# The expert stage of a graph, mixer and mixture-of-experts block, rebuilt around one table of turns

## What is computed

```python
# N = 1250 tokens, D = 768, G*E = 32 experts, M = 384; two groups of the 4, two experts of each
glog = xf @ Wg + bg                       # top 2 of 4 groups, softmax of their logits
elog = take_along_axis(elog_all, gidx)    # top 2 of 8 experts in each, softmax again
comb[n, expert] = ggate * egate           # 4 of 32 entries of a token are not zero
h = gelu(x[n] @ W1[e] + b1[e])            # for the tokens of an expert
out = sum_e comb[n, e] * (h @ W2[e] + b2[e])
```

## Time and profile before

| | us |
|---|---|
| three runs, median (lowest to highest) | 2640.47 (2627.52 to 2644.08) |
| profiled execution, first to last instruction | 2648.0 |
| of it from the first real `ex_PH` to the last | 563.3 |

### The profile page before, as it was taken

One profiled execution on the slowest core, in us unless ns is written; L12 is line 12 of the kernel. 1 busy time (PEld: TensorE's weight loads), 2 busy tenths in 40 slices (PEclk: granted clock), 3 DMA queues, 4 the chain that ended last, 5 costly groups with the idle time before them and its releaser, 6 DMA issues. The chain is left out here.

```text
span 2648.0 us, 32969 instructions
## 1 busy us (share of the span) xinstructions
PE 2149.9 (81%) x8696; PEld 1415.3 (53%) x8697; DVE 1172.5 (44%) x2660; ACT 443.9 (17%) x721; POOL 190.2 (7%) x205
## 2 busy tenths in 40 slices
PE   2998998596999922599999799539846888988997
PEld 1666665452555512488888455215543555555554
DVE  3113213133666626579888011056434444444442
ACT  1232112100111112122222000000000222222221
POOL 0000000000000000000000000000001222222222
PEclk9998998897999955799999899769956999989999
DMA  4001200113000045222322411321152777778653
GB/s 162 40 0 63 81 0 36 70 44 117 23 23 24 22 150 184 112 111 95 115 99 81 161 62 55 130 80 48 31 206 81 207 210 225 219 240 257 163 122 66
DMA packets 104535, 278.90 MB, mean 105 GB/s; under 512 B 8053, under 2 KB 53159, under 8 KB 103067
## 3 DMA queue, kind: packets, MB, share of 16 engines
q1 hardware_dynamic: 82727, 210.86, 22.6%
q0 software_dynamic: 15184, 55.37, 9.1%
q10 hardware_dynamic: 6560, 11.86, 1.2%
HBM read 214.49 MB, written 63.57 MB: 105 GB/s over the span
## 5 line engine op out<-in xcount | busy, mean ns | idle before, releaser
L1179 PE MATMUL gat_Z<-h,gat_wt 125*125 125x256 f32 (+1 forms) x1600 | 356.4, 382 | 40.0 <-DVE gat_wt L1095 40.0
L1179 PEld LDWEIGHTS gat_Z<-h,gat_wt 125*125 125x125 f32 x1600 | 299.3, 189 | 85.7 <-DVE gat_wt L1095 40.5
L2034 PE MATMUL ex_PH<-ex_w,ex_xT 128*128 x636 | 240.3, 532 | 24.2 <-DVE ex_xT L1883 14.5
L542 PE MATMUL mix_G<-mix_w,mix_xs 128*125 128x384 f32 x720 | 243.4, 489 | 0.0
L2023 PE MATMUL ex_PY<-ex_w,ex_hT 128*128 (+1 forms) x660 | 223.7, 489 | 15.9 <-POOL ex_hT L1838 14.8
L825 PE MATMUL count_G<-gnn_w,xnT 128*125 (+1 forms) x480 | 214.3, 596 | 18.5 <-issue 18.5
L1329 PE MATMUL gat2p_Y<-gat2p_w,gat2p_hT 128*125 128x384 f32 x640 | 209.3, 491 | 12.2 <-DMA gat2p_w<-in_L_gnn_W 12.2
L2034 PEld LDWEIGHTS ex_PH<-ex_w,ex_xT 128*128 128x128 f32 x636 | 126.9, 207 | 109.7 <-issue 48.2
L2023 PEld LDWEIGHTS ex_PY<-ex_w,ex_hT 128*128 128x128 f32 x660 | 126.1, 191 | 105.0 <-issue 18.8
L542 PEld LDWEIGHTS mix_G<-mix_w,mix_xs 128*125 128x125 f32 x720 | 133.4, 189 | 85.1 <-issue 2.6
L1329 PEld LDWEIGHTS gat2p_Y<-gat2p_w,gat2p_hT 128*125 128x125 f32 x640 | 121.3, 190 | 99.8 <-issue 14.9
(11 more groups left out here) (292 smaller groups left out, 2456.9 us busy)
## 6 DMA issues: line engine op xcount, KB each, us to landing
ex_w<-in_L_ffn_W SPq DMA_DIRECT2D x64, 1152.0 KB, 8.0
gat_cnt<-c_dram SPq DMA_DIRECT2D x50, 610.4 KB
h1T_dram<-gat_oT ACTq DMA_DIRECT2D x40, 250.0 KB, 2.0
gat2p_hT<-h1T_dram SPq DMA_DIRECT2D x10, 1000.0 KB, 4.8
mix_w<-in_L_mix_qkv_w SPq DMA_DIRECT2D x6, 1152.0 KB
ct_dram<-count_out SPq DMA_DIRECT2D x40, 157.0 KB, 2.2
mix_w_slice<-in_L_gnn_W SPq DMA_DIRECT2D x6, 1024.0 KB, 11.0
gat2p_w<-in_L_gnn_W SPq DMA_DIRECT2D x4, 1536.0 KB, 13.7
```

The lines of the kernel that those rows point to most:

```text
L542: last = pe.matmul(G[c][:], xs[b][:, k, :], w[:, k, c, :], start=(k == 0), stop=(k == KD - 1))
L1179: last = pe.matmul(Z[b][j][:], wt[b][:, s, :], h[:, s, bass.ds(hd, 1), j * HC:(j + 1) * HC + j], start=(s == 0), stop=(s == NT - 1))
L2034: last = pe.matmul(PH[:], xT[:, k, :], w1[:, bass.ds(b, 1), k, :], start=(k == 0), stop=(k == KD - 1))
```

## The change

- `route_phase` makes a table of turns once, by small products on PE in a new PSUM tile `TB`: for each turn the expert (`etab`) and the offset of its first place (`offs`), and the number of turns (`total`). The nine chained DVE steps that made `ntile` and `tstart` go, and so do two copies into `codes`, which POOL now makes.
- First product: the weights `w1` are held still, 128 by 128, and the 128 tokens of `xT` stream. Eighteen matmuls of 128 columns take the place of six of 384. The result is already turned, so that the transposes `ex_TH` and their copy go; ACT takes Gelu straight from PSUM with the bias as a column per partition (`b1T`, loaded once), in three pieces.
- `find` works by the table: one DVE operation makes `Q` from `posm` and `offs`, with the expert loaded into a register (`etab`). Row numbers and gates are kept in four slots each (`ids`, `gate`).
- DVE, ACT and POOL have one loop over all turns, in place of loops over experts. POOL issues the gather of turn i+2 ahead of the scatter of turn i. Before, it issued the scatter first.
- A first activation `warm` loads ACT's table once. The host stores `W1`, `W2` and `b1` in the order in which a partition reads them.

The core of the diff, with the new programs of the engines in `expert_phase`:

```diff
+            def gather(n):
+                pool.wait_ge(idx_ready, n + 1)
+                if not (isinstance(n, int) and n == 0):
+                    pool.wait_ge(x_turned, n)
+                    pool.wait_ge(gathered, n * 16)
...
+            def scatter(n):
+                pool.wait_ge(y_d, n + 1)
+                pool.wait_ge(y_a, n + 2)
+                pool.wait_ge(idS_ready, n + 1)
...
+            with pool.Fori(0, end) as i:
+                gather(i + 2)
+                scatter(i)
...
+            def find(n):
+                e = expert_of(dve, n)
...
+                    dve.wait_ge(ids_done, n)
+                dve.scalar_tensor_tensor(Q[:], posm[:, :, bass.ds(e, 1)].to_broadcast([P, NT, SLOT]),
+                                         offs[:, bass.ds(at, 1)],
+                                         iot[:].unsqueeze(1).to_broadcast([P, NT, SLOT]),
+                                         ALU.subtract, ALU.is_equal).then_inc(q_ready, 1)
+
+            def indices(n):
+                slot = slot_of(dve, n)
+                dve.wait_ge(ids_done, n + 1)
+                dve.wait_ge(y_a, n)
+                dve.tensor_copy(cod[:], PI[:]).then_inc(ids_copied, 1)
+                dve.wait_ge(ids_copied, n + 1)
+                dve.scalar_tensor_tensor(gate[:, slot], cod[:, 5:6], cod[:, 4:5], cod[:, 3:4], ALU.add, ALU.add)
...
+            with dve.Fori(0, end) as i:
+                indices(i + 2)
+                find(i + 3)
+                turn_x(i + 1)
+                second(i)
...
             def second(n):
-                act.wait_ge(gemm2, n)
-                act.wait_ge(g_ready, n)
-                act.activation(y[:, 384:768], PY[1][:], ACT.Copy, scale=gS[:]).then_inc(y_a, 1)
...
+                slot = slot_of(act, n)
+                act.wait_ge(idx_ready, n + 1)
+                act.wait_ge(added, n * 16)
+                act.wait_ge(gemm2, n + 1)
+                act.activation(y[:, 384:768], PY[1][:], ACT.Copy, scale=gate[:, slot]).then_inc(y_a, 1)
+
+            act.wait_ge(consts, 2)
+            act.activation(warm[:], pad[:], ACT.Gelu)
+            act.sem_inc(h_gelu, KM)
+            act.sem_inc(y_a, 1)
...
+            with act.Fori(0, end) as i:
+                first(i)
+                turn_x(i + 1)
+                second(i)
...
+            def first(n, b):
+                pe.wait_ge(xT_d, n + 1)
+                pe.wait_ge(xT_a, n + 1)
+                for m in range(KM):
+                    pe.wait_ge(h_gelu, n * KM + (m + 1))
+                    for k in range(KD):
+                        last = pe.matmul(PH[m][:], w1[:, b, k, m * 128:(m + 1) * 128], xT[:, k, :],
+                                         start=(k == 0), stop=(k == KD - 1))
+                    last.then_inc(gemm1, 1)
...
+                        with pe.Fori(0, count) as _:
+                            n = pe.snap(turn)
+                            find(n + 2)
+                            first(n, b)
+                            turn_x(n + 1)
+                            second(n, b)
+                            pe.reg_add(turn, turn, 1)
```

More of the change, by code:

```diff
@@ L1700, in _ @@
             step(dve.tensor_scalar(posm[:], posm[:], -1.0, None, ALU.add))
[L1702 to L1710, removed]
+            dve.wait_ge(tab_pe, 3)
+            dve.tensor_copy(etab[:], TB[0:1, 128:128 + NTAB])
+            dve.scalar_tensor_tensor(offs[:], TB[0:P, 256:256 + NTAB], -float(SLOT), turn[:, 1, :], ALU.mult, ALU.add)
             for t in range(NT):
@@ L1730, in _ @@
             pe.matmul(PT[:], ones[:], rhs, start=True, stop=True).then_inc(counted, 1)
+            for t in range(NT):
+                last = pe.matmul(TB[0:NE, 0:1], sele[:, t * NG:(t + 1) * NG, :].rearrange("p a e -> p (a e)"),
+                                 ones[:, 0:1], start=(t == 0), stop=(t == NT - 1))
+            last.then_inc(tab_pe, 1)
             pe.wait_ge(comb_ready, 1)
@@ L1861, in _ @@
[L1861 to L1867, removed]
+            gather(0)
+            gather(1)
+            end = turns(pool)
+            with pool.Fori(0, end) as i:
+                gather(i + 2)
+                scatter(i)
+            pool.wait_ge(gathered, end * 16 + 32)
@@ new lines, in second @@
+            def second(n):
+                slot = slot_of(dve, n)
+                dve.wait_ge(added, n * 16)
+                dve.tensor_scalar(idS[:], ids[:, slot], 1.0, None, ALU.mult).then_inc(idS_ready, 1)
+                dve.wait_ge(gemm2, n + 1)
+                dve.tensor_scalar(y[:, 0:384], PY[0][:], gate[:, slot], None, ALU.mult).then_inc(y_d, 1)
+            dve.wait_ge(consts, 2)
+            find(0)
+            end = turns(dve)
+            indices(0)
+            find(1)
+            indices(1)
@@ new lines, in _ @@
+            find(1)
+            turn_x(0)
+            with pe.register("ex_turn_pe") as turn:
+                pe.reg_mov(turn, 0)
+                with pe.Fori(0, NE // NB) as i:
+                    for b in range(NB):
+                        pe.wait_ge(w_loaded[b], i * 32 + 32)
+                        count = pe.value_load(ntile[0:1, bass.ds(i * NB + b, 1)], min_val=1, max_val=NT)
+                        with pe.Fori(0, count) as _:
[5 more added lines that the diff above has]
+                            pe.reg_add(turn, turn, 1)
```

354 lines of the change are left out of this document (134 added, 220 removed).

## The result

The changed kernel takes 2929.43 us, the median of four runs (2922.78 to 2932.21), against 2640.17 (2627.52 to 2644.08) for the kernel before, of which there are now four runs too. That is 1.109 times as long, with an interval of 1.106 to 1.112: 289 us slower, where the forecast was 278.

The account below looks back on a forecast made before the run. PE's own chain was taken to bound a turn of 11.05 us. With 51 turns of 16.6 us, fill -7.6, routing +1 and drain +1, 2648.0 became 2925.5; less 7.5 gave 2918 us, range 2800 to 3000.

Parts of the forecast that it names:

- The likeliest case: Expert stage: DVE's wait in `indices` puts its round behind PE's and PE's clock falls; 2918 us, chance 0.74.
- The forecast's own marks: Profile after: PE idle 5 to 6 us before `ex_PH`, released by `ex_xT`; `ex_cod` released by `ex_y`; PEclk under 0.95.
- The gap: Each turn, `ex_PY` to next `ex_PH`: PE has only `ex_PI` while DVE's serial chain runs, 5.61 us (4.5 to 6.5).
- The clock: Each turn, PE runs at a lower clock after standing idle: 2.3 us lost (1.3 to 3.1).
- PE's work: Each turn at full clock: first product 3.96, transposes 0.66, second product 3.87, tail 0.16; 8.65 us.
- The rival of loads in series: First product: each weight load adds to its stream, 7.7 us for 3.96; 3108 us, chance 0.02.
- Gathers and scatters: POOL's transfers in the expert stage: 37.5 us of gather waits go, scatter lands in time, fewer DMAs in flight cost nothing.
- Fill and start: Expert stage up to first real `ex_PH`: dummy round goes, 14.3 us for 21.9, a gain of 7.6 (4 to 9).
- Routing: `route_phase`: nine DVE steps and two copies go, about eight small steps and three PE waits come; +1 us (-2 to +4).
- The sum: Whole kernel: 2648.0 - 7.6 + 1 + 1 + 51 x (16.6 - 11.05) = 2925.5 us; less 7.5 gives 2918.
- drain: End of the expert stage: length kept but for DVE's order, where y comes last; +1 us.
- The faster rival: `indices`: wait on `y_a` met before DVE comes, rounds overlap, a turn of 9.25 us; 2543 us, chance 0.05.

Follow-up runs that it names:

- The filled gap: Changed kernel with 20 matmuls whose result nobody reads put behind each turn's second product on PE, the wait kept: 2845.05 us, ratio 1.077.
- the kernel with the lower count: Changed kernel with the wait on `y_a` in `indices` asking for one turn less (n - 1): 2536.05 us, ratio 0.960.
- three kernels with gaps of 5.05 to 6.11 us: Changed kernel, 2929.43 us; the same with only `turn_x(i + 1)` ahead of `indices` on DVE, 2922.82; or only `find` behind PE's first product, 2926.38.

## Why the forecast was right, step by step

The likeliest case came in: 2929 us for 2918, inside the range, with the mechanism as read. The count that `indices` waits for is that of the same turn, and lowering it by one takes 393 us off. The forecast's own marks are all there: `ex_cod` is released by ACT's `ex_y`, PE is idle before each `ex_PH` but for `ex_PI`, the gathers are not waited for, the clock is 0.80. Two read otherwise: PE is released by `ex_Q` and not by `ex_xT`, and its idle time is 4.6 us, not 5 to 6, since `ex_PI` fills more of the gap.

- **The gap**, forecast 5.61 us, is 6.11. Its first parts are within 0.2 each (0.84 for 0.83, 0.20 for 0.23, 1.15 for 1.2, 0.71 for 0.9, 1.55 for 1.5). The term that was off is the last: 0.95 for copy, `ex_PI` and start. I took `ex_PI` at the 0.40 it had with work ahead of it and put it beside the copy. It takes 1.35, and with 0.15 on either side 1.66 in all. This alone is +0.7 a turn, and -0.2 came from the load.
- **The clock**, forecast 2.3 us a turn, is 2.0 in the turn shown: 10.99 us of PE's work for 8.98 at the full clock. The filled gap gave 1.6 of it back in the mean.
- **PE's work**, forecast 8.65 us, is 8.98 in the filled gap, with the modelled tail of each product, 0.33 more; it is 9.05 a turn with `ex_PI` in the kernel with the lower count. The rival of loads in series is out.
- **Gathers and scatters**: no wait is left, as forecast. It was less obvious than I made it. It hangs on the gather's place in POOL's queue, which by itself is worth 400 us in the kernel with the lower count.
- **Fill and start**: forecast -7.6, measured -28.1. The fill's own part was right, -6.7. Missed were SP's issues in the phase before, 16.5 us, which the change shortens and which I had not looked at because its lines are called from outside the stage; and 4.9 that the program was ahead already, within what this point moves from one execution to the next. **Routing**, +1, measured 0.
- **The sum**: a turn of 17.07 for 16.6 (gap +0.5, clock -0.3, work +0.3) is 51 x 0.47 = 24 us more, the start is 20.5 less, routing and drain 1 less each. So 2927.3 in the profiled execution for a forecast of 2925.5 is two errors of over 20 us that cancel, not a sum that was exact. The other 9.6 of the 11.4 us between forecast and median: the span of before lay 7.5 over its median, that of after 2.1 under its own. Some of this is no spread, since a time on record is longer than the span of the same execution (2929.07 for 2927.3). And that gap and clock add up at all is in part luck: three kernels with gaps of 5.05 to 6.11 us have one turn of 17.03 to 17.07, so the two terms are not independent there, as the sum takes them to be.
- **The faster rival**, 2543 us for a wait that is met early, came out at 2536, and there too errors cancel: a turn of 9.46 for 9.25 is 11 us more, the first `ex_PH` came 24.1 us earlier for 7.6, and the drain took 22.3 us for 30.1.

## What to carry to other kernels

Where engines run rounds of a loop against each other, write down for each wait which round's work of the other engine it asks for. A count that is one too high turns engines that overlap into one chain, and no busy share in a profile of before can show it. When PE is released late, ask for every instruction behind the wait, not the one that the profile names: here the copy and `find` each sufficed to hold PE, and each alone moved gained nothing. And look at the time and not only at the gap: a gap that was 1.06 us shorter left the turn as it was. A loop two turns ahead needs all of its parts: row numbers early, gather ahead of scatter, and nothing of the current turn's end in front of either.

## What the runs showed of the hardware

- Ten small bf16 matmuls (`ex_PI`) mostly take 0.40 us where their operand has been ready for a while and PE comes to them out of other work, and 1.31 to 1.41 where the operand has only just come, in stages with a mean clock of 0.99 as of 0.80. Why is not shown.
- PE at work in a gap, with useless matmuls, shortens the kernel: 84 us by 20 matmuls a turn, with the granted clock from 0.80 to 0.98.
- A shorter gap need not pay: 5.05 us of idle PE for 6.11 with `ex_PI` in it left the time as it was, since `ex_PH` behind it took 6.76 for 6.30, and 7.20 at the end of the stage. The turn stayed at 17.03 to 17.07 us in three kernels.
- Twelve issues of weights and biases on SP took 23.7 us with rows in pieces and 12.3 with one piece per partition; in the second case the slowest gather landed after 10.2 us and not 8.6. That the one caused the other is not shown.
